# Cross-attention: subtraction for 64 channels on GpSimd and moved by transfers of the sync engine, exponentials first on ScalarE

## The reference

```python
# x: context, layernormed over 192 channels;  latents: layernormed
q = latents @ Wq.T
k = concat(x @ Wk.T, latents @ Wlk.T)
v = concat(x @ Wv.T, latents @ Wlv.T)
# 4 heads of 64
qn = rmsnorm(q, qn_g) * 64 ** -0.5
kn = rmsnorm(k, kn_g)               # k / max(|k| / 8, 1e-8)
attn = softmax(mask(qn @ kn.T))
out = (attn @ v) @ Wo.T + bo
```

## Time and profile before

| | us |
|---|---|
| median of 3 runs (lowest, highest) | 522.01 (521.84, 523.51) |
| the profiled execution's own time | 520.81 |
| its span, first to last instruction | 519.0 |

### The profile page before, as it was taken

How to read it: one execution, slowest core, us unless ns; L and a number is a source line. 1 busy time by engine, 2 the same in 40 slices (tenths; PEclk the granted TensorE clock), 3 DMA queues, 4 the chain that set the end, 5 groups by cost and what they waited for, 6 DMA issues and landing times.

```text
span 519.0 us, 6624 instructions
## 1 busy us (share of the span) xinstructions
PE 431.1 (83%) x2042; PEld 334.5 (64%) x2042; DVE 405.3 (78%) x969; ACT 237.8 (46%) x547; POOL 250.3 (48%) x264
## 2 busy tenths in 40 slices
PE   3786557779799889887998988887997877899996
PEld 0364335567677677675786867774474765678885
DVE  5847799999999999999988896625659556887776
ACT  0238645267466564664654744331233125335551
POOL 5451956658558557576484553001431232445550
PEclk9999988889999999999899999899999988889999
DMA  8605842022141041222200000920000000000001
GB/s 248 179 1 148 237 135 56 2 90 53 51 141 50 3 141 50 76 67 58 90 3 1 1 1 15 406 97 0 0 2 0 1 0 0 1 1 1 0 2 41
DMA packets 23976, 31.80 MB, mean 61 GB/s; under 512 B 2955, under 2 KB 19653, under 8 KB 23941
## 3 DMA queue, kind: packets, MB, share of 16 engines
q1 hardware_dynamic: 23940, 31.38, 19.6%
HBM read 30.69 MB, written 0.52 MB: 60 GB/s over the span
## 4 chain that ended last, share of the span: by engine, by line
DVE 34%; PE 30%; POOL 21%; issue 8%; ACT 4%; DMA 2%; SPq 1%; DVEq 0%; POOLq 0%; ACTq 0%
PE bank L573 29%; POOL kr L483 12%; DVE kss L1397 5%; DVE arena L1409 4%; DVE arena L1445 3%; DVE split_b L1388 3%; POOL crs L448 3%; DVE cst L1334 2%; DVE arena L1604 2%; DVE arena L1618 1%; DVE kguard L1400 1%; POOL split_b L472 1%; DVE big L1319 1%; POOL cguard L449 1%; DMA mask_in<-in_p_mask 1%
## 5 line engine op out<-in xcount | busy, mean ns | idle before, releaser
L573 PE MATMUL bank<-keyq,split_b 128*128 128x512 f32 (+2 forms) x724 | 171.0, 384 | 21.2 <-DVE split_b L1678 6.7
L573 PEld LDWEIGHTS bank<-keyq,split_b 128*128 128x128 f32 (+1 forms) x724 | 124.7, 194 | 51.3 <-issue 18.0
L483 POOL TENSOR_TENSOR kr<-kguard,neg_half 128x8 f32<-128x8 f32 (+1 forms) x56 | 94.4, 1686 | 103.5 <-DVE kguard L1400 103.1
L573 PE MATMUL bank<-arena 128*128 128x193 f32 (+4 forms) x528 | 103.4, 340 | 18.5 <-ACT arena L1133 9.0
L573 PEld LDWEIGHTS bank<-arena 128*128 128x128 f32 (+2 forms) x528 | 86.9, 195 | 31.1 <-issue 13.9
L1126 ACT ACTIVATE arena<-bank 128x512 f32<-128x512 f32 (+1 forms) x56 | 31.5, 563 | 59.9 <-PE bank L573 59.4
L573 PE MATMUL bank<-split_b,keyq 128*128 128x512 f32 x204 | 51.7, 405 | 0.1
L1409 DVE TENSOR_TENSOR arena<-bank,kr 128x512 f32<-128x512 f32 (+1 forms) x56 | 36.1, 645 | 19.3 <-POOL kr L483 19.1
L1388 DVE TENSOR_TENSOR split_b<-arena,split_b 32x256 fp32r<-32x256 f32 (+1 forms) x112 | 48.0, 428 | 2.5
L573 PEld LDWEIGHTS bank<-split_b,keyq 128*128 128x128 f32 x204 | 39.1, 197 | 8.0 <-DVE split_b L1669 0.2
L472 POOL TENSOR_TENSOR split_b<-arena,split_b 128x256 fp32r<-128x256 f32 (+1 forms) x56 | 38.2, 682 | 10.1 <-ACT split_b L1109 10.0
(11 more groups left out here) (222 smaller groups left out, 620.5 us busy)
## 6 DMA issues: line engine op xcount, KB each, us to landing
arena<-in_ctx SPq DMA_DIRECT2D x16, 576.0 KB, 4.4
arena<-in_p_ctxT SPq DMA_DIRECT2D x8, 800.5 KB, 6.7
arena<-in_p_ctxT SPq DMA_DIRECT2D x8, 400.2 KB, 7.1
arena<-in_p_experts SPq DMA_DIRECT2D x1, 2688.0 KB, 18.4
arena<-in_p_experts SPq DMA_DIRECT2D x1, 2304.0 KB, 12.2
arena<-in_p_experts SPq DMA_DIRECT2D x1, 1536.0 KB, 6.4
X<-in_x SPq DMA_DIRECT2D x1, 512.0 KB, 3.7
arena<-in_t_Wlkv SPq DMA_DIRECT2D x1, 512.0 KB, 7.0
```

Source lines behind the costliest of these rows:

```text
L483: pool.tensor_tensor(kr[0:r, n % 2, 0:k], kg_[0:r, n % 2, 0:k], neg_half[0:r, 0:4 * k].rearrange("p (t h) -> p t h", h=H), ALU.pow).then_i ...
L573: return nc.tensor.matmul(out_, l, r, start=start, stop=stop, skip_group_check=shared)
```

## The change

- `split_side` on DVE is gone. In its place POOL, right after `split_rest(n)`, computes the low part of all 64 channels in one instruction into a small buffer `side_low` (64 partitions, two turns), and SP moves it to partitions 96 to 127 of slots 2 and 3 with two transfers (`move_side`). `keys(n)` waits for these, semaphore `side_in[n % 3]`.
- On ACT the high part of the 64 channels becomes `split_small(n)`, with a semaphore of its own and the wait for `sd_in`. The exponentials come first in a step, and `split_small` after `square_keys` where g = 5.
- SP works step by step: `move_side(u+2)` in each step, the context loads in steps 0 and 4, the turned context in steps 1 and 2, `spread_sd` in step 4, the mixer's weights three to a step in batch 0, `wx2a` in step 7.
- `cguard` is gone; L1400 takes `cve` with a factor instead. The factor 64 ** -0.5 moves from `qkg` to `evac_latent_scores`.

```diff
+            def move_side(n):
+                k = 256 if n % NG < NG - 1 else TAIL
+                sp.wait_ge(xs_side, n + 1)
+                for j in range(2):
+                    sp.dma_start(xs[n % 3][96:P, 2 + j, 0:k].bitcast(F32), side_low[32 * j:32 * j + 32, n % 2, 0:k].bitcast(F32)).then_inc(side_in[n % 3], 16)
...
-            for b in range(B):
-                if b + 2 < B:
+            move_side(0)
+            move_side(1)
+            for u in range(groups):
+                b, g = divmod(u, NG)
+                if u + 2 < groups:
+                    move_side(u + 2)
+                if g == 0 and b + 2 < B:
...
-                if b + 1 < B:
-                    load_turned(b + 1)
-                if b + 2 < B:
+                if g in (1, 2) and b + 1 < B:
+                    load_turned(b + 1, g - 1)
+                if g == 4 and b + 1 < B:
+                    spread_sd(b + 1)
+                if g == 4 and b + 2 < B:
...
-                then(pool.tensor_scalar(cguard[:, k, of], cve[:, k, of], 1e-16, None, ALU.mult))
...
                 pool.tensor_tensor(v[:, 1, 0:k], raw[:, 0], v[:, 0, 0:k].bitcast(F32), ALU.subtract).then_inc(xs_rest, 1)
+                pool.wait_ge(xs_small, n + 1)
+                if n >= 2:
+                    pool.wait_ge(side_in[(n - 2) % 3], 32 * ((n - 2) // 3 + 1))
+                pool.tensor_tensor(side_low[:, n % 2, 0:k], raw[0:SMALL, 1], v[0:SMALL, 2, 0:k].bitcast(F32), ALU.subtract).then_inc(xs_side, 1)
...
-                pe.wait_ge(xs_side, n + 1)
+                pe.wait_ge(side_in[n % 3], 32 * (n // 3 + 1))
...
+            def split_small(n):
+                b, g = divmod(n, NG)
+                if g == 0:
+                    act.wait_ge(sd_in[b % 2], 32 * (b // 2 + 1))
+                k = 256 if g < NG - 1 else TAIL
+                A(xs[n % 3][0:96, 2:4, 0:k], ctxT[b % 2][0:96, 1:2, 256 * g:256 * g + k].broadcast_to([96, 2, k]), ACT.Copy).then_inc(xs_small, 1)
...
+                if 0 <= u - SUM < groups:
+                    exponentials(u - SUM)
                 if u + 2 < groups:
                     split_high(u + 2)
+                    if g != 5:
+                        split_small(u + 2)
                 if u < groups:
                     scale_context(u)
-                if 0 <= u - SUM < groups:
-                    exponentials(u - SUM)
                 if u < groups:
                     square_keys(u)
+                if g == 5 and u + 2 < groups:
+                    split_small(u + 2)
...
-            def split_side(n):
-                dve.wait_ge(xs_split, n + 1)
...
-                for j in range(2):
-                    last = V.tensor_tensor(v[96:P, 2 + j, 0:k], side_[32 * j:32 * j + 32], v[32 * j:32 * j + 32, 2 + j, 0:k].bitcast(F32), ALU.subtract)
-                last.then_inc(xs_side, 1)
...
-                if u + 2 < groups:
-                    split_side(u + 2)
```

More of the change, by code:

```diff
@@ L177, in build @@
         csd = sb("csd", [P, FULL + 1])
-        cguard = sb("cguard", [P, 2, FULL + 1])
         sdT = sb("sdT", [FULL + 1, P])
+        side_low = sb("side_low", [SMALL, 2, 256], F32R)
         sd_part = sb("sd_part", [FULL + 1, 2, P], F32R)
@@ L350, in _ @@
             sp.wait_ge(pool_const, 1)
-            load_turned(0)
+            mixer_weights = (
+                    (wo[:], a["t_Wo"].rearrange("(c p) n -> p c n", p=P)),
+                    (bo[:], a["L0_xattn_bo"].rearrange("(o d) -> o d", o=1)),
+                    (sums[:], a["c_sums"]), (pick[:], a["c_pick"]), (headsel[:], a["c_head"]),
+                    (wx0[:], a["t_W_x0"].rearrange("(c p) n -> p c n", p=P)),
+                    (wx2b[:], a["t_W_x2"][P:160, :]),
+                    (wr[:], a["t_W_r"].rearrange("(c p) n -> p c n", p=P)),
+                    (wk[:], a["t_W_k"].rearrange("(c p) n -> p c n", p=P)),
+                    (ww1[:], a["t_W_w1"].rearrange("(c p) n -> p c n", p=P)),
+                    (ww2[0:64, :], a["t_W_w2"]), (ww2[64:65, :], a["L0_attn_b_w2"].rearrange("(o d) -> o d", o=1)),
+                    (wv[:], a["t_W_v"].rearrange("(c p) n -> p c n", p=P)),
+                    (wg[:], a["t_W_g"].rearrange("(c p) n -> p c n", p=P)),
+                    (wo2[:], a["t_W_o"].rearrange("(c p) n -> p c n", p=P)),
+                    (gatew[:], a["t_gate_w"].rearrange("(c p) n -> p c n", p=P)),
+                    (ebias[:], a["L0_ffn_e_bias"].rearrange("(o d) -> o d", o=1).broadcast_to([P, NE])),
+                    (before[:], a["c_before"].broadcast_to([P, NE * NE])),
+                    (gbefore[:], a["c_gbefore"].broadcast_to([P, 16])),
+            )
+            for c in range(2):
+                load_turned(0, c)
             load_context(1, 0)
@@ L1180, in _ @@
             evac_queries()
-            split_high(0)
-            split_high(1)
+            for n in range(2):
+                split_high(n)
+                split_small(n)
             for j in range(4):
```

55 lines of the change are left out of this document (15 added, 40 removed).

## The result

The changed kernel takes 524.28 us in the median (522.99 to 526.96) against 522.93 for the kernel before on the same chip (519.43 to 523.9), 19 runs each. The ratio is 1.0038, with a 95% interval of 1.0021 to 1.0056: slower by 1.1 to 2.9 us. The forecast was 526.2. The profiled execution of the changed kernel took 526.96 (span 525.2), 2.7 above its median and the slowest of the 19, so absolute sums from the trace are a little long. Two of the twelve executions of experiment e4 took 708 and 2293 us and are left out of its numbers.

A forecast was written before the change was run, and what follows sets the result against it. Bound: the loop of GpSimd's kr and VectorE. Batches 2 to 5 +1.2, 0 and 1 +3.3, 6 +0.8, 7 +1.1, start -2.2: +4.2 us on 522.01, hence 526.2 (521 to 530; with rivals 506 to 532).

The forecast's parts named there:

- The mechanism of the collisions: VectorE's maximum, starting 0.07 us after GpSimd's side_low, loses 0.51 us after groups 2, 4 and 5: 1.5 per batch.
- Batches 2 to 5: Relief on VectorE -2.7, collisions +2.8, GpSimd's order +0.2: +0.3 us each, +1.2 together.
- The collision in the last group: After group 6, the maxima L1426 and L1428 meet split_rest and side_low: 0.8 us per batch, bounds 0.3 and 1.1.
- Start: Before the first kr, four split_side pieces for groups 0 and 1 leave VectorE: -2.2 us.
- batches 0 and 1: Shorter kr and less lateness against collisions and GpSimd's order: +1.8 and +1.5 us, together +3.3.
- is still inside: Transfer pairs for side_low: one queued behind an 800 KB load, 1 to 3 us later, is still covered, costing nothing.
- (D): Rival: late context load or transfer pair, once a pair takes over some 7 us; 1 us per batch, 533; chance 0.13.
- Batches 6 and 7: Collisions outweigh relief in the last two batches: +0.8 us in batch 6, +1.1 in batch 7 up to group 53.
- (B): Rival: VectorE gets in first, the maximum runs free and GpSimd waits where it has time: 505; chance 0.20.
- (C): Rival: about half of the collisions, the order tipping in some groups only: 516; chance 0.17.
- (E): Rival: TensorE, 30.5 us of work per batch, becomes the bound, capping gains at 4.7 per batch; no chance given.
- The costs at nothing: Second context load (other bound 1 us per batch), ScalarE's new order, SP's order and smaller edits: all counted zero.

The follow-up runs named there:

- e4: Changed kernel with ScalarE's old order put back (exponential behind the splits, both splits of a group together): 526.2 us, ratio 1.0065.
- e2: Changed kernel with the mixers' weights loaded one per step from the third batch on, not three per step in the first: 522.9 us, ratio 1.0011.
- e12: Changed kernel with ScalarE's old order put back, the same edit as e4, run again for its trace: 526.15 us, ratio 1.0073.
- e1: Changed kernel with GpSimd's new subtraction waiting until VectorE's running maximum (in some steps the shift) is done: 522.13 us, ratio 0.999.
- e9: Changed kernel with a tiny GpSimd memset between split_rest and the new subtraction, so that the maximum starts first: 525.19 us, ratio 1.0064.
- e6: Changed kernel with subtraction behind the maximum, weights' loads from third batch, step 4 reordered, two groups' low parts per batch back on VectorE: 504.2 us, ratio 0.9657.
- e11: Kernel before with only ScalarE's new order (exponential first, small split by itself): 521.9 us, ratio 0.999.
- e10: Kernel before, split_side kept, with a one-input GpSimd multiplication by 1.0 (64 x 256) added behind split_rest: 537.39 us, ratio 1.0285.

## Why the prediction came out as it did

**The sum and the sign.** I had +4.2 us; the medians give +1.35, the interval 1.1 to 2.9, so the size was too large by a factor of 1.4 to 4. Up to the end of the last `kr` the traces are 2.76 apart (323.01 and 325.77). Of these, 2.1 belong to one late pair of transfers in batch 1, which I had put at nothing, and e2, which doesn't have it, can't be told from the kernel before. Batches 2 to 5, on which most of the working was spent, came out on the other side of zero. So the direction came out right by luck as much as by the sum. The rest of the gap between the two profiled executions lies behind the last `kr`: 199.4 us to the end against 196.0 in the kernel before. It doesn't belong to the change, since e2, with the same code in this stretch, has 196.0 too. The windows below are of the changed kernel, with a granted clock of 0.72, and of e2, with 1.00.

```profile
345.00:360.00 15.00, 12.68 (x52) 8.15 (x50) 5.41 (x17) 1.19 (x4) 1.72 (x4) 0.72 0.00 0
```

```profile
345.00:360.00 15.00, 11.86 (x63) 8.63 (x62) 6.54 (x18) 2.43 (x7) 2.45 (x4) 1.00 0.00 1
```

**The mechanism of the collisions was right.** VectorE's relief was eaten by collisions that start about 0.1 us after GpSimd (0.07 forecast), `kr` is 1.64 nearly everywhere, L1428 waits for it in 50 of 56 groups, and a batch takes 34.9 us, just below the 35 to 36 I had named. One comparison in the prediction was wrong: rule and row don't give the same 0.51. A maximum held from 73.52 for the whole of L472, until 74.17, would lose 0.65 us; the row has 0.51.

**Batches 2 to 5: +0.3 forecast, -0.3 measured.** By intervals of batch 3, forecast and measured: g = 4, -0.9 and -1.04 (L1428 late by 0.47, not 0.6); g = 3, +0.51 and +0.48; g = 5 and 6, +0.28 and +0.25 each; g = 1, +0.2 and +0.34; g = 0, -0.25 and -0.39; g = 2, +0.2 and -0.15. The two terms that I had mis-sized most are those taken from far-off rows. The collision in the last group was set at 0.8:

```profile
186.68 0.49 DVE L1445 TENSOR_TENSOR arena<-arena 65x256 f32<-65x256 f32 x1
186.84 0.92 POOL L490 TENSOR_TENSOR side_low<-arena,split_b 64x256 fp32r<-64x256 f32 x1
187.20 0.85 DVE L1447 TENSOR_TENSOR arena<-arena 64x256 f32<-64x256 f32 x1
```

The two maxima (L1445 and L1447 are the former L1426 and L1428) lose 0.5 together over the 0.42 that each took before. And in g = 2 GpSimd's rows of the kernel before and of the changed one are:

```profile
162.73 0.77 POOL L449 TENSOR_SCALAR cguard<-cve 128x7 f32<-128x7 f32 x1
```

```profile
163.42 0.69 POOL L462 TENSOR_SCALAR cve<-cmv 128x7 f32<-128x7 f32 x1
```

The maximum does hold L462 (0.69 instead of 0.28 in this batch), by 0.4 and not 0.5. But `cguard` had cost 0.77 in that place and not its mean of 0.56, so its going gave more than I had credited, and `csd` behind it is 0.12 shorter. In g = 1, 0.14 above the forecast, it is the other way round: `csd` takes 0.49 (158.44) beside a piece of the shift, where it took 0.20.

**Start, and batches 0 and 1: +1.1 forecast to the end of the second batch, +2.33 measured.** The first `kr` ends 1.4 us earlier, not 2.2; in e12, e2, e1 and e9, with nearly the same work ahead of it, 1.0, 1.9, 2.4 and 2.8, so the term was right within what this stretch varies. Batch 0 behind it cost 0.8, not 1.8. Batch 1 cost 2.9, not 1.5, and e2 shows that 2.1 of these are the late pair; without it batch 1 costs 0.8. The step that failed is the one by which a pair that comes 1 to 3 us later behind a big load "is still inside". The pair took 4.9 us from the end of the subtraction (74.24) to the products (79.17), ahead of which TensorE had no other work. That is 2.0 more than the 2.9 forecast, so as late as I had granted, and it wasn't inside. What failed is the slack of about 4 us, read from batch 4. The subtraction was itself late, as it had waited 0.66 us for ScalarE's split behind `sd_part` (72.79). The products took 4.61 us, at a granted clock of 0.50, so that `kr` started 6.2 us after their start (85.41) and not 4. And the last two intervals of batch 0 (3.96 and 4.02) are together 1.2 shorter than in batch 3. By these numbers each of them alone would have fitted into the slack. I had also asked only when the mixers' weights are needed ("until 350 us"), not what stands behind them in the queues. The threshold of 7 us in rival (D) was too high here by 2 for the same reasons.

**Batches 6 and 7:** +0.8 forecast and +0.55 measured; +1.1 and +1.1 (the terms named for batch 7 add up to 1.0).

**The rivals.** (B) at 505 was priced as if only the maximum could collide. e9 shows that when VectorE gets in first, the shift is held in the maximum's place wherever it comes next; only g = 3 gains, 0.5 a batch. (C) didn't come either: g = 3, 5 and 6 are longer by 0.25 to 0.48 in every batch from 2 to 5. (D) came once, in batch 1, for 2.1 us, and in full when e1 moved the subtraction: then the waits for `in_ctx` were 16 us. (E) never bound here; in batch 3 of e6 TensorE is busy for 29.9 of 32.3 us, so little is left above it.

**The costs at nothing.** Statistics waiting for the context: 3.5 us of waits, 1.9 of them in batch 0, where L1428 is 1.04 late. ScalarE's order: nothing on the kernel before, by e11; on the changed kernel it stays open. The sync engine's order step by step, the going of `cguard` and the smaller edits (L1419's operands, the moved scale) were not tried by themselves, so their terms are read from rows alone.

## What to carry to other kernels

Where GpSimd and VectorE alternate in a closed loop, place the GpSimd instruction beside a VectorE instruction with one input in SBUF, not 0.1 us before or after one with two: winning the race moves the loss to the next one, if that has two inputs as well. When a small transfer gets a deadline of a few us, look for every large load that the same queue issues in the steps before it, whatever its own deadline, and work out the slack where the loads stand, not in an even stretch. And when a cost is taken away with little gain, read who waits next before giving it up: e1 looked like a failure (522.1); the weights' loads moved, the order in step 4 that its waits pointed to, and two groups back on VectorE made it 504.2.

## What the runs showed of the hardware

- Instructions with two inputs in SBUF, on GpSimd and VectorE, take turns: the maximum 0.69, then the subtraction 1.23 of which some 0.5 is waiting, then the shift 1.23 with as much (e9). The sum of squares, with one input, kept its 0.68 when the same subtraction began 0.17 us into it (188.30 and 188.47 in e1).
- On GpSimd an instruction with one input (64 x 256) is held for a whole maximum when it comes 0.02 us second (1.38), but holds a maximum for only 0.16 when it comes 0.08 us first (e10).
- GpSimd's `kr` (128 x 8) takes 1.64 us beside the statistics, 1.87 when VectorE starts `split_side`'s two-input pieces with it, and 2.06 in the row shown of e6, where VectorE's pieces fall within it.
